# Softmax attention with a latent: the product of probabilities and latent as three one-pass products on a high part and a rest

## The reference

```
q = rope(x @ wq)                          # 16 heads of 128
c_kv = x @ w_down                         # latent, 128 wide
k, v = split(c_kv @ w_up); k = rope(k)
scores = where(causal, q @ k.T * Dh**-0.5, -inf)
out = (softmax(scores) @ v) @ wo
```

## Time and profile before

| | us |
|---|---|
| median of three runs | 1581.57 (1573.38 to 1584.28) |
| profiled execution | 1589.05 |
| its span, first to last instruction | 1586.1 |
| PE busy in the span | 1451.1 (91%) |
| DVE busy | 916.5 (58%) |
| ACT busy | 579.3 (37%) |
| POOL busy | 555.5 (35%) |
| product of probabilities and latent (line 1681), PE busy | 155.1 (512 records) |
| mean granted TensorE clock | 0.959 |

### The profile page before, as it was taken

One profiled execution on the slowest core, in us unless ns is written; L12 is line 12 of the kernel. 1 busy time (PEld: TensorE's weight loads), 2 busy tenths in 40 slices (PEclk: granted clock), 3 DMA queues, 4 the chain that ended last, 5 costly groups with the idle time before them and its releaser, 6 DMA issues.

```text
span 1586.1 us, 23380 instructions
## 1 busy us (share of the span) xinstructions
PE 1451.1 (91%) x7914; PEld 1116.5 (70%) x7914; DVE 916.5 (58%) x2166; ACT 579.3 (37%) x1373; POOL 555.5 (35%) x483
## 2 busy tenths in 40 slices
PE   7899999999999999989999889999999999776991
PEld 6676767777777777666776568878888788663560
DVE  4576767676767676743333255656657565655214
ACT  4344444444444444631211043334333333331330
POOL 2754545455555555100112123333423512203123
PEclk9999999999999999999999989999999999878996
DMA  5000000000003000010000010020020001954994
GB/s 169 7 4 7 4 7 3 7 3 7 3 7 81 0 0 0 1 60 0 1 0 0 0 67 15 7 74 8 8 73 7 14 8 42 254 172 143 295 245 120
DMA packets 68217, 76.33 MB, mean 48 GB/s; under 512 B 14205, under 2 KB 55445, under 8 KB 68149
## 3 DMA queue, kind: packets, MB, share of 16 engines
q1 hardware_dynamic: 56789, 58.49, 13.0%
q10 hardware_dynamic: 8288, 12.22, 2.5%
q0 software_dynamic: 3072, 4.72, 1.5%
HBM read 66.22 MB, written 9.21 MB: 48 GB/s over the span
## 4 chain that ended last, share of the span: by engine, by line
PE 79%; DVE 8%; POOL 4%; issue 3%; ACT 2%; DMA 2%; another core or an unknown queue 1%; POOLq 0%; DVEq 0%; ACTq 0%
PE ps L1594 37%; PE ps L1681 9%; PE ps L1703 9%; PE ps L1688 6%; PE ps L1733 4%; PE ps L1823 4%; PE ps L2029 2%; DVE acc L1148 1%; PE ps L1900 1%; PE ps L2094 1%; PE ps L1890 1%; PE ps L2111 1%; PE ps L1705 1%; DMA sums_dram<-rows 1%
## 5 line engine op out<-in xcount | busy, mean ns | idle before, releaser
L1102 DVE TENSOR_REDUCE mx<-ps 128x1 f32<-128x128 f32 (+3 forms) x256 | 125.6, 491 | 156.4 <-PE ps L1705 151.3
L608 POOL TENSOR_TENSOR qk<-q,ksb 128x512 f32<-128x512 f32 x64 | 82.6, 1290 | 304.0 <-ACT q L831 215.3
L1703 PE MATMUL ps<-kT,qT 128*128 128x128 f32 (+3 forms) x512 | 175.1, 451 | 3.2 <-ACT probs L747 3.2
L747 ACT ACTIVATE probs<-ps,nm 128x128 f32<-128x128 f32 (+3 forms) x256 | 135.0, 527 | 114.9 <-DVE nm L1105 107.2
L1046 DVE TENSOR_TENSOR prod<-ps,rope_sb 128x1024 f32<-128x1024 f32 x128 | 150.8, 1219 | 19.5 <-PE ps L1594 14.0
L1681 PE MATMUL ps<-pT,c_tok 128*128 128x512 f32 (+3 forms) x512 | 155.1, 446 | 0.7 <-ACT pT L690 0.7
L690 ACT ACTIVATE pT<-ps 128x256 f32<-128x256 f32 (+3 forms) x256 | 93.5, 441 | 153.2 <-PE ps L1733 153.2
L486 POOL TENSOR_TENSOR qT<-prod 64x512 f32<-64x512 f32 x64 | 81.5, 1273 | 179.2 <-PE ps L1705 93.8
L1681 PEld LDWEIGHTS ps<-pT,c_tok 128*128 128x128 f32 x512 | 92.1, 190 | 67.2 <-issue 30.6
L1688 PE MATMUL ps<-U,oT 128*128 (+1 forms) x512 | 124.6, 386 | 0.7 <-ACT oT L690 0.7
L486 POOL TENSOR_TENSOR kT<-prod 64x512 f32<-64x512 f32 x64 | 81.5, 1273 | 121.6 <-DVE prod L1046 113.9
(11 more groups left out here) (249 smaller groups left out, 2586.1 us busy)
## 6 DMA issues: line engine op xcount, KB each, us to landing
eg<-in_L_ffn_w_gate_dram SPq DMA_DIRECT2D x16, 704.0 KB
eg<-in_L_ffn_w_up_dram SPq DMA_DIRECT2D x16, 704.0 KB
ed<-in_L_ffn_w_down_dram ACTq DMA_DIRECT2D x10, 640.0 KB
ksb<-ks_dram SPq DMA_DIRECT2D x16, 256.0 KB, 3.2
ed<-in_L_ffn_w_down_dram SPq DMA_DIRECT2D x6, 640.0 KB
rows_dram<-rows ACTq DMA_DIRECT2D x4, 640.0 KB, 4.0
acc<-in_L_attn_x_dram SPq DMA_DIRECT2D x4, 512.0 KB
wq_in<-in_L_attn_wq_dram SPq DMA_DIRECT2D x8, 256.0 KB, 2.8
```

The costliest lines, as they stand in the source:

```text
L608: nc.gpsimd.tensor_tensor(qk[:], q3[:], ksb[b % 2][:], ALU.mult).then_inc(qk_ready, 1)
L747: nc.scalar.activation(probs[hh][:, off:off + (i + 1) * P], ps[:, BS + i % 2, 0:(i + 1) * P], ACT.Exp, bias=nm[:, hh, i:i + 1], scale=SCAL ...
L1102: nc.vector.tensor_reduce(mx[:, hh, i:i + 1], ps[:, BS + i % 2, 0:(i + 1) * P], AX_X, ALU.max).then_inc(max_ready, 1)
L1703: pe.matmul(ps[:, bank, 0:(i + 1) * P], qT[:, hh, b, i * P:(i + 1) * P], kT[:, hh, b, 0:(i + 1) * P], start=True, stop=False)
```

## The change

`pv_and` no longer multiplies in plain float32 where 256 columns or more are moved. The latent `c_tok` is kept as a high part and a rest, the transposed probabilities as `pT` (high) and `pT_low` (rest); for the first three key tiles there are three one-pass products each. The last key tile, with 128 columns, stays in plain float32, from `c_end` and `pT_end`. The rests of the probabilities are four new subtractions on VectorE at each step's end, and the low products wait for them (`ptlo_ready`). ScalarE's last copy of a step becomes two. The score scale is multiplied into the query weights when they are split, and no longer in the exponential; the maximum is written negated by the reduction itself, and its separate negation goes. To make room, `lb_in`, `la_in` and `ldn` move to where the rope products lie, so SP issues their transfers only after the last rotation (`load_small`).

```diff
-        c_tok = place("c_tok", 68, [P, TILES, DH])
+        c_tok = [place("c_tok0", 68, [P, TILES, DH], F32R), place("c_tok1", 199, [P, TILES, DH], F32R)]
+        c_end = place("c_end", 170, [P, BATCH, DH])
...
-        pT = place("pT", 164, [P, TPB, T])
+        pT = place("pT", 164, [P, TPB - 1, T], F32R)
+        pT_low = place("pT_low", 185, [P, TPB - 1, T], F32R)
+        pT_end = place("pT_end", 207, [P, P])
...
+            sp.wait_ge(roped, 4 * STEPS * PAIRS)
+            load_small()
...
-                copy(wq[0][:], wq_in[:]).then_inc(wq_hi, 1)
+                nc.scalar.activation(wq[0][:], wq_in[:], ACT.Copy, scale=SCALE).then_inc(wq_hi, 1)
...
-                for i in (2, 3):
-                    act.wait_ge(transposed, 3 * s + i)
-                    copy(pT[:, 0:i + 1, i * P:(i + 1) * P],
-                         ps[:, BW + i - 2, 0:(i + 1) * P].rearrange("p (k q) -> p k q", q=P)).then_inc(pt_copied, 1)
+                act.wait_ge(transposed, 3 * s + 2)
+                copy(pT[:, :, 2 * P:3 * P], ps[:, BW, 0:3 * P].rearrange("p (k q) -> p k q", q=P)).then_inc(pt_copied, 1)
+                act.wait_ge(transposed, 3 * s + 3)
+                copy(pT[:, :, 3 * P:4 * P], ps[:, BW + 1, 0:3 * P].rearrange("p (k q) -> p k q", q=P))
+                copy(pT_end[:], ps[:, BW + 1, 3 * P:4 * P]).then_inc(pt_copied, 1)
...
+            for b in range(BATCH):
+                dve.wait_ge(ctok_ready, b + 1)
+                at = slice(b * TPB, (b + 1) * TPB)
+                rest(c_tok[1][:, at, :], ps[:, 4 + b, :].rearrange("p (i l) -> p i l", i=TPB), c_tok[0][:, at, :]).then_inc(clo_ready, 1)
...
-                    nc.vector.tensor_reduce(mx[:, hh, i:i + 1], ps[:, BS + i % 2, 0:(i + 1) * P], AX_X,
-                                            ALU.max).then_inc(max_ready, 1)
-                    dve.wait_ge(max_ready, 4 * s + i + 1)
-                    nc.vector.tensor_scalar(nm[:, hh, i:i + 1], mx[:, hh, i:i + 1], -SCALE, None,
-                                            ALU.mult).then_inc(negmax_ready, 1)
+                    nc.vector.tensor_reduce(nm[:, hh, i:i + 1], ps[:, BS + i % 2, 0:(i + 1) * P], AX_X, ALU.max,
+                                            negate=True).then_inc(negmax_ready, 1)
...
                 nc.vector.reciprocal(rinv[:, hh, :], rs[:, hh, :]).then_inc(rinv_ready, 1)
+                dve.wait_ge(pt_copied, 3 * s + 1)
+                rest(pT_low[:, 0, 0:2 * P], ps[:, BW + 2, 0:2 * P], pT[:, 0, 0:2 * P])
+                rest(pT_low[:, 1, P:2 * P], ps[:, BW + 2, 2 * P:3 * P], pT[:, 1, P:2 * P]).then_inc(ptlo_ready, 1)
+                for i in (2, 3):
+                    dve.wait_ge(pt_copied, 3 * s + i)
+                    q = slice(i * P, (i + 1) * P)
+                    rest(pT_low[:, :, q], ps[:, BW + i - 2, 0:3 * P].rearrange("p (k q) -> p k q", q=P), pT[:, :, q]).then_inc(ptlo_ready, 1)
...
-                for k in range(TPB):
-                    last = pe.matmul(ps[:, BO, k * P:T], c_tok[:, b * TPB + k, :], pT[:, k, k * P:T],
-                                     start=k == 0, stop=k == TPB - 1)
+                for k in range(TPB - 1):
+                    for h in range(2):
+                        pe.matmul(ps[:, BO, k * P:T], c_tok[h][:, b * TPB + k, :], pT[:, k, k * P:T],
+                                  start=k == 0 and h == 0, stop=False)
+                pe.matmul(ps[:, BO, 3 * P:T], c_end[:, b, :], pT_end[:], start=False, stop=False)
+                pe.wait_ge(ptlo_ready, 3 * s + 3)
+                for k in range(TPB - 1):
+                    last = pe.matmul(ps[:, BO, k * P:T], c_tok[0][:, b * TPB + k, :], pT_low[:, k, k * P:T],
+                                     start=False, stop=k == TPB - 2)
```

More of the change, by code:

```diff
@@ L353, in _, with load_small @@
                 sp.dma_start(gu_in[:, :, w, :], io["L0_ffn_W_" + name].rearrange("(k p) n -> p k n", p=P)).then_inc(gu_loaded, 16)
[L354 to L363, removed]
+            def load_small():
+                for w, name in enumerate(("gate", "up")):
+                    sp.dma_start(lb_in[0:R0, w, :], io["L0_ffn_sB_" + name]).then_inc(lb_loaded, 16)
+                    sp.dma_start(lb_in[R0:NL, w, :], io["L0_ffn_B_" + name].rearrange("e r n -> (e r) n")).then_inc(lb_loaded, 16)
+                sp.dma_start(la_in[:, :, 0:E0], io["L0_ffn_W_router"].rearrange("(k p) n -> p k n", p=P)).then_inc(la_loaded, 16)
+                for w, name in enumerate(("gate", "up")):
+                    at = E0 + w * NL
+                    sp.dma_start(la_in[:, :, at:at + R0], io["L0_ffn_sA_" + name].rearrange("(k p) n -> p k n", p=P)).then_inc(la_loaded, 16)
+                    for k in range(KD):
+                        sp.dma_start(la_in[:, k, at + R0:at + NL].rearrange("p (e r) -> p e r", r=R0),
+                                     io["L0_ffn_A_" + name].rearrange("e (k p) r -> k p e r", p=P)[k]).then_inc(la_loaded, 16)
             for lo, hi, size in ((0, 4, 115), (4, 6, 114)):
@@ L714, in _ @@
                 act.wait_ge(c_turned, b + 1)
-                copy(c_tok[:, b * TPB:(b + 1) * TPB, :],
-                     ps[:, 4 + b, :].rearrange("p (i l) -> p i l", i=TPB)).then_inc(ctok_ready, 1)
+                copy(c_tok[0][:, b * TPB:(b + 1) * TPB, :], ps[:, 4 + b, :].rearrange("p (i l) -> p i l", i=TPB))
+                copy(c_end[:, b, :], ps[:, 4 + b, (TPB - 1) * P:T]).then_inc(ctok_ready, 1)
             for j in range(4):
@@ L747, in exps @@
                     nc.scalar.activation(probs[hh][:, off:off + (i + 1) * P], ps[:, BS + i % 2, 0:(i + 1) * P], ACT.Exp,
-                                         bias=nm[:, hh, i:i + 1], scale=SCALE,
+                                         bias=nm[:, hh, i:i + 1],
                                          accum_out=rs[:, hh, i:i + 1]).then_inc(probs_ready, 1)
@@ L1033, in split_wq @@
                 dve.wait_ge(wq_hi, g + 1)
-                rest(wq[1][:], wq_in[:], wq[0][:]).then_inc(wq_lo, 1)
+                nc.vector.scalar_tensor_tensor(out=wq[1][:], in0=wq_in[:], scalar=SCALE, in1=wq[0][:].bitcast(F32),
+                                               op0=ALU.mult, op1=ALU.subtract).then_inc(wq_lo, 1)
             def split_wk(g):
@@ L1648, in turn_wv @@
                         pe.wait_ge(ctok_ready, 4)
+                        pe.wait_ge(clo_ready, BATCH + 4)
                     for i in range(4):
@@ L1723, in step @@
                         if i == 0:
-                            pe.wait_ge(pt_copied, 3 * s - 2)
+                            pe.wait_ge(ptlo_ready, 3 * s - 2)
                         if i >= 2:
```

19 lines of the change are left out of this document (9 added, 10 removed).

## The result

| | before | after |
|---|---|---|
| median, us | 1581.67 (1573.38 to 1584.28, 4 runs) | 1559.26 (1557.0 to 1562.32, 4 runs) |
| profiled execution, us | 1589.05 | 1562.32 |
| its span, us | 1586.1 | 1560.6 |
| first score product of the attention loop, us | 49.96 | 50.10 |
| start of the last output product of the attention loop, us | 685.58 | 666.41 |

The ratio is 0.9861, with a 95% interval of 0.9835 to 0.9886: the change saves 22.4 us. The forecast was 1571 us in a range of 1556 to 1587. The sign and the range held; the gain is twice the 11 us of the sum.

A forecast was written before the change was run, and what follows sets the result against it. TensorE was taken to bound the attention loop. Seven pairs and the first step's correction gave -16.0 us, the last pair +5.0, together -11.0 from the 1581.57 median: 1571 us, range 1556 to 1587.

The forecast's parts named there:

- The product: Probabilities times latent on TensorE: 2.26 us becomes 1.81, net gain 0.39 a step after 0.06 for the extra copy.
- rival C: In the product, 384 columns cost as much as 512, or the extra copy 0.2 more: 1583 us; chance 0.14.
- VectorE's part: VectorE's step chain: negations go, rests add 1.76 us, fourth maximum at 6.0, 0.15 later; query-split step +0.15.
- The key-split step: Step after the query split: rests start behind late adds, the last bound by its copy; -0.15 us.
- Rival B: VectorE hides everything, also in split steps and the last pair: 29 us gained, 1553 us; chance 0.14.
- A: The forecast itself for the whole kernel: 11 us gained, between 1562 and 1580 us; chance 0.61.
- the signs of being wrong: TensorE waiting for exponentials in ordinary steps, 384 columns far from 0.176 us, or a last pair that does not lengthen.
- The tightest place: Ahead of a step's third score product: first exponentials ready at 2.7 us, TensorE free at 2.77, room 0.1 us.
- rival D: Rests make VectorE the bound ahead of the third score product: at 2.6 us for the rests, 1618 us; chance 0.08.
- rival E: Eleven weight loads instead of eight don't hide between TensorE's products of unlike length: 28 us, 1599 us; chance 0.03.
- The last pair: Loop's last pair: VectorE's extra work comes behind the rests, five steps 1.2 us longer each; +5.0 us in all.
- The small loads: Small weight loads wait on SP until the last rotation, yet arrive before ScalarE needs them: no cost.

The follow-up runs named there:

- the held GpSimd: Kernel before, with GpSimd's rotations in the two split steps held until VectorE's weight rest is done: 1576.34 us, ratio 0.9977.
- the negation alone: Kernel before, with the scale folded into the query weights and the maximum written negated, old four-pass product kept: 1577.61 us, ratio 0.9982.
- the product alone: Kernel after, with the scale back in the exponential and the separate negation back: 1570.96 us, ratio 0.9929.
- the best kernel: Kernel after, with VectorE's adds ahead of the weight splits and the last pair's extra VectorE work behind the following step's second maximum: 1551.87 us, ratio 0.9803.

## Why the gain was twice the forecast

- **The product: right in its place, 0.09 us a step too good.** Forecast 1.81, measured 1.90, so a step TensorE bounds gained 0.31 and not 0.39. The 384-column products came out at 0.17 to 0.18, where 0.176 was interpolated. What was missed is the first product of the high group: single records start at 428.44, 428.77, 429.01, so the first costs 0.33 and the next 0.24. The old product had the same extra (0.53 for the first 512-column record, 0.43 for the next), but the price list came from a stream without it. The ScalarE copy more cost the 0.06 taken for it: the product starts at t = 0.98 and not 0.92. The 42 ordinary steps of seven pairs by 0.08 are 3.4 us less gain than the sum had; rival C, 384 columns at the price of 512, falls.
- **"VectorE's part", the failed step.** The sum kept the weight rest at the 1.42 us of the earlier trace rows and put the fourth maximum at 6.0, from which +0.15 followed for the query-split step. Measured: rest 0.89, fourth maximum 5.44, step -1.02. That step is 1.17 better than forecast, over seven pairs 8.2 us, nearly the whole miss. Two terms made it. The rest's length is 0.53 of the 1.17, shown by its rows and by the held GpSimd. The other 0.64 is the chain ahead of the rest: it was forecast 0.15 later than before, and the rest starts 0.49 earlier; 0.56 of it stands already at the fourth maximum. I had added the durations of rows one by one. In the trace an instruction of this chain starts 0.08 us before the one ahead has ended (399.75 + 0.61 is 400.36, the next starts at 400.28), and the four rests take 1.47 us from their start to the first maximum's (398.28 to 399.75), not 1.76. Neither part of the change brings the rest forward like this alone: with the negation alone it starts 0.19 earlier, since the maxima then wait for scores behind the old product; with the product alone 0.46 later. It takes both, which is why their 2.7 and 11.4 us do not add up to 19.3.
- **The key-split step** gained 0.39 and not 0.15, 1.7 us over seven pairs. It was taken to be held by late adds and the rests behind them; TensorE has no idle time in it after, and with the product alone it has the same 10.14. So it is a step that TensorE bounds.
- **Rival B.** The measured 22.4 us lie between A's 11 and B's 29, but VectorE does not hide everything: the wait for adds still stands in the query-split step (0.34), and the last pair did get longer. And none of the signs of being wrong that the prediction named came true. None of them looked at the term that failed, the length and start of the weight rest.
- **The tightest place held.** TensorE has no idle time ahead of the third score product in an ordinary step: the first exponential and its sum were out at t = 2.34 and TensorE came at 2.88, so the room was 0.5 us and not 0.1, as the rests ended at t = 1.49. So rival D did not happen; the rests did not double, and with them taken out ordinary steps kept their length (8.80 and 10.20).
- **Weight loads hide (rival E).** Eleven loads a step instead of eight, and the product costs what its columns cost.
- **The last pair: mechanism right, size 5.0 for 2.9.** The step behind the statistics is as forecast: third score product at t = 4.13 (4.3 forecast), output product at 5.91 (6.0), 3.47 us behind it (3.48). But I gave its price to all five steps; in the others the first maximum starts at t = 2.93 (647.35 after 644.42), since the rests end 0.4 earlier. The five cost 1.12, 0.47, 0.75, 0.75 and about 1.1, together 4.2 instead of 6.0. The third step, forecast +0.15, gained 0.30.
- **The small loads cost nothing, as said.** They are issued from 619.08 on, ahead of their use by ScalarE, and no engine waits for them; the timeline of SP:

```profile
619.08 0.29 SPq L358 DMA_DIRECT2D lb_in<-in_L_ffn_sB_gate_dram  x1
...
625.68 0.52 SPq L384 DMA_DIRECT2D ldn<-in_L_ffn_B_down_dram  x1
```

The errors in sum: -8.2 and -1.7 in the split steps, +3.4 in the ordinary ones, -2.1 in the last pair make -8.6, so 19.6 where the loop shows 19.3; the rest is what seven pairs make of hundredths.

## What to carry to other kernels

A step that ends on a wait for a second engine is worth a look at that engine's whole chain, by the start times of its instructions and not by the sum of their durations. A duration read from a step in which a third engine runs is a price of that meeting, not of the instruction: before it goes into a sum, look at what GpSimd does at its start, in each place where it stands. And the order of a short list decides more than the arithmetic in it: moving adds ahead of a rest that waits for another engine gave 12.3 us in the medians (11.5 in the loop) with no work removed, more than half of what the whole change gave. Last, the start of a loop moved by 2 us between executions here: a gain inside it is read between two marks in the trace, not from the time at which it ends.

## What the runs showed of the hardware

**A VectorE subtraction with both inputs in SBUF meets GpSimd.** The same 128x512 rest took 0.69 us with GpSimd idle or when it started just ahead of a rotation, and 0.89, 1.27, 1.33, 1.42, 1.57 and 1.80 us when a rotation was running at its start, with 0.35, 0.71, 0.78, 0.86, 1.02 and 1.25 us of that rotation left: the rest ends 0.54 to 0.56 us after the rotation does, wherever it began. That is 0.14 less than the 0.69 it takes alone. Behind the adds (the best kernel) it is the same: a rest at 448.75 beside a rotation that ends at 449.93 took 1.73. The rotation behind it is stretched in turn, from 1.28 to 1.60 or 1.80 us. The rests with one input in PSUM show none of it: in the kernel after the four took 0.43, 0.28, 0.55 and 0.55 us beside a rotation (from 398.28) and without one (from 369.47). The Trainium skill (SBUF — State Buffer, Who interferes with whom) says that VectorE with two SBUF inputs and GpSimd exclude each other; the trace agrees.

**A delay can pay for itself.** Because of that, taking work out of VectorE's list (the four rests) gained 0.7 us in the whole loop: 5.6 us won in the last pair, and 4.9 given back by seven meetings that became 0.7 us longer.

**The first product of a group that TensorE waits for.** The high group starts when ScalarE's copies are done. Its first 512-column product costs 0.33 us to the next start, the one behind it 0.24; in plain float32, before, 0.53 and 0.43. The weight load of that first product starts together with it (both at 399.24), while the next loads start a product ahead of theirs. That this is the reason is read from the rows and not tested. A wait in the program is not enough: the low group has one too, long met, and its first product and the 128-column product ahead of it take 0.45 us together (400.40 to 400.85), which is what the prices of records inside a group add up to (2 x 0.11 + 0.24).
